# Three stages of a metaformer kernel, their engine programs written without loops

## The reference, cut to what matters

```
x = x + attention(layernorm(x))            # 7x7 windows, shifted, 4 heads
t = t + experts(layernorm(t))              # softmax router over 8 experts, the best 2 mixed
x = x + focal(layernorm(x))                # below
t = t + recurrence(layernorm(t))           # batch norm, then 3136 steps of sigmoid(wx_t + y @ V.T)

experts:  expert_out = einsum('bnd,edc->bnec', x, expert_w) + expert_b
          out = sum over the top 2 of p_k * expert_out[k]
focal:    y = x @ Wf + bf                  # q, context and 4 gates
          three depthwise convolutions with gelu, each times its gate, and a global term
          x_out = q * (ctx_all @ Wh + bh)
          x_out = layernorm(x_out) * gamma + beta
          x_out = x_out @ Wp + bp
```

## Time and profile before

| what | value |
|---|---|
| time, median of 3 runs | 8981.09 us (8978.25 to 9027.3) |
| time of the profiled execution | 8979.28 us |
| its span, first to last instruction | 8977.5 us |
| mean granted TensorE clock | 0.973 |
| PE, DVE, POOL, ACT busy | 90%, 70%, 64%, 50% of the span |
| attention, to 1840 us | 1840 us |
| experts, 1840 to 3862 us | 2022 us |
| focal input, 3862 to 4455 us | 593 us |
| convolution, 4455 to 6070 us | 1615 us |
| focal output, 6070 to 7097 us | 1027 us |
| recurrence, 7097 us to the end | 1880 us |

### The profile page before, as it was taken

One profiled execution on the slowest core, in us unless ns is written; L12 is line 12 of the kernel. 1 busy time (PEld: TensorE's weight loads), 2 busy tenths in 40 slices (PEclk: granted clock), 3 DMA queues, 4 the chain that ended last, 5 costly groups with the idle time before them and its releaser, 6 DMA issues. The chain is left out here.

```text
span 8977.5 us, 330977 instructions
## 1 busy us (share of the span) xinstructions
PE 8051.4 (90%) x112719; PEld 4838.4 (54%) x112719; DVE 6262.3 (70%) x21127; ACT 4513.2 (50%) x12517; POOL 5701.4 (64%) x6959
## 2 busy tenths in 40 slices
PE   7999999978889898779799999988888788888888
PEld 6777777744444444357544444436666555555554
DVE  8999999979999999878656666656777622222222
ACT  5666666645555555469733333335555433333333
POOL 8999999968888888778622222225666644444444
PEclk9999999989999999989999999999999899999999
DMA  1222222211111111258844554538777422222221
GB/s 52 57 57 57 58 58 58 59 53 54 54 54 54 51 53 54 69 183 301 286 163 164 180 181 164 180 124 214 200 203 200 121 55 55 56 56 56 56 55 53
DMA packets 797656, 955.86 MB, mean 106 GB/s; under 512 B 323100, under 2 KB 661825, under 8 KB 773584
## 3 DMA queue, kind: packets, MB, share of 16 engines
q1 hardware_dynamic: 797264, 952.06, 34.7%
HBM read 574.81 MB, written 453.35 MB: 115 GB/s over the span
## 5 line engine op out<-in xcount | busy, mean ns | idle before, releaser
L982 PE MATMUL moe_pe_out<-moe_we,moe_xnT 128*128 128x512 f32 x3136 | 1530.2, 621 | 232.3 <-DVE moe_acc L876 224.9
L1587 PE MATMUL conv_pc<-conv_c,conv_toep 64*64 64x416 f32 (+1 forms) x6896 | 1335.6, 534 | 4.2 <-ACT conv_c L1488 2.7
L778 ACT ACTIVATE moe_scaled<-moe_pe_out,moe_gate 128x128 f32<-128x128 f32 x3136 | 892.5, 368 | 792.8 <-PE moe_pe_out L982 791.1
L2287 ACT ACTIVATE rec_yT<-rec_ph 128x32 f32<-128x32 f32 x3136 | 618.4, 197 | 1251.5 <-PE rec_ph L2408 1251.5
L1443 POOL TENSOR_TENSOR conv_g<-conv_c,conv_gate 128x896 f32<-128x896 f32 x128 | 365.3, 2854 | 1212.2 <-DVE conv_out L1557 1174.6
L982 PEld LDWEIGHTS moe_pe_out<-moe_we,moe_xnT 128*128 128x128 f32 x3136 | 558.5, 195 | 1032.1 <-issue 1023.8
L298 POOL TENSOR_SCALAR att_xn<-att_xin,att_mv,att_rstd 128x128 f32<-128x128 f32 x1024 | 1007.1, 997 | 54.2 <-POOL att_rstd L294 54.2
L2408 PE MATMUL rec_ph<-rec_yT,rec_vt 128*32 128x32 f32 x25080 | 853.1, 207 | 196.6 <-ACT rec_yT L2287 121.8
L2334 DVE COPY rec_xT<-rec_pin 128x512 f32<-128x512 f32 x196 | 135.6, 692 | 1250.5 <-PE rec_pin L2380 1250.5
L2408 PEld LDWEIGHTS rec_ph<-rec_yT,rec_vt 128*32 128x32 f32 x25080 | 506.5, 108 | 647.5 <-ACT rec_yT L2287 609.9
L1587 PEld LDWEIGHTS conv_pc<-conv_c,conv_toep 64*64 64x64 f32 (+1 forms) x6896 | 487.9, 144 | 604.8 <-issue 535.2
(11 more groups left out here) (210 smaller groups left out, 19573.4 us busy)
## 6 DMA issues: line engine op xcount, KB each, us to landing
conv_toep<-rows_dram SPq DMA_DIRECT2D x32, 2304.0 KB, 13.9
c<-foc_cs SPq DMA_DIRECT2D x32, 1792.0 KB, 10.9
conv_cin<-c SPq DMA_DIRECT2D x32, 1792.0 KB, 8.9
ctx_all<-conv_out SPq DMA_DIRECT2D x32, 1792.0 KB, 7.0
att_xin<-x_windows SPq DMA_DIRECT2D x512, 98.0 KB
moe_xin<-x SPq DMA_DIRECT2D x112, 448.0 KB, 3.5
x<-moe_acc SPq DMA_DIRECT2D x112, 448.0 KB, 2.7
foc_xin<-x SPq DMA_DIRECT2D x32, 1568.0 KB, 8.3
```

The costliest lines, as they stand in the source:

```text
L778: ins = act.activation(scaled[:, b, e, :], pe_out[:, b, 1, e * C:(e + 1) * C], ACT.Identity, scale=g)
L982: pe.matmul(pe_out[:, b, half, :], xnT[:, n.slot(2), t, :], we[:, half * 4:half * 4 + 4, :].rearrange("d e c -> d (e c)"), start=True, sto ...
L1587: return pe.matmul(image_pairs(pc[k], half)[m0:m1, :, i0:i1], w, tile[r0:r1, images(half), i0 + away:i1 + away], start=start, stop=(rows ! ...
L2287: act.activation(yT[:, a, cs], ph[:, a, cs], ACT.Sigmoid).then_inc(moved, 1)
```

## The change

The five `run_steps` calls of each of experts, focal input and focal output (15 in all) become calls of a new function that writes every step out. No instruction on data, no wait and no transfer is added, removed or moved within a program; waits and addresses of the former loop steps are constants. `run_steps` stays as it is for the other three stages.

```diff
+def straight_steps(count, unroll, step):
+    for n in range(count):
+        step(Step(0, unroll, n), n, n - count)
...
 # expert_stage: SP, POOL, ACT, DVE, PE
-            run_steps(sp, N, U, step, 5)
+            straight_steps(N, U, step)
...
-            run_steps(pool, N, U, step, 4)
+            straight_steps(N, U, step)
...
 # focal_input_stage: SP, POOL, ACT, DVE, PE
-            run_steps(sp, N, U, step, 4 * NG)
+            straight_steps(N, U, step)
...
-            run_steps(dve, N, U, step, AHEAD)
+            straight_steps(N, U, step)
...
 # focal_output_stage: SP, POOL, ACT, DVE, PE
-            run_steps(sp, N, U, step, 3 * NG)
+            straight_steps(N, U, step)
...
-            run_steps(dve, N, U, step, AHEAD)
+            straight_steps(N, U, step)
```

More of the change, by code:

```diff
@@ L796, in step @@
                         norm(n + 2)
-            run_steps(act, N, U, step, 4)
+            straight_steps(N, U, step)
         @block.vector
@@ L948, in step @@
                     layer_stats_end(n + 3)
-            run_steps(dve, N, U, step, 4)
+            straight_steps(N, U, step)
         @block.tensor
@@ L996, in step @@
                             logits(n + 1, 1)
-            run_steps(pe, N, U, step, 4)
+            straight_steps(N, U, step)
 ROW = 64
@@ L1150, in step @@
                     norm(n + 9, first + 9)
-            run_steps(pool, N, U, step, AHEAD)
+            straight_steps(N, U, step)
         @block.scalar
@@ L1197, in step @@
                 context(n, first)
-            run_steps(act, N, U, step, AHEAD)
+            straight_steps(N, U, step)
         @block.vector
@@ L1309, in step @@
                     turn(n + 8, first + 8)
-            run_steps(pe, N, U, step, AHEAD)
+            straight_steps(N, U, step)
 T_ALL = P * sum(BLOCKS)
```

## The result

The kernel before ran in 8979.67 us (median, 8973.55 to 9027.3), the changed one in 8765.99 us (8764.0 to 8767.61). The ratio is 0.9751, with an interval of 0.9717 to 0.9784: 2.5% faster. I had predicted 8799 us, 8765 to 8850. Applied to the 8981.09 us that the prediction started from, the ratio gives 8757 us. The direction and most of the size were right, and yet the result lies at the low edge of the range or just beyond it: 33 us of gain are missing in my sum.

A forecast was written before the change was run, and what follows sets the result against it. Experts was read as a chain over VectorE; it and focal output stall at loop turns. Terms -85 - 100 + 3 = -182 us on 8979.3 gave 8797, plus 1.8 for the runs' median: 8799 us, range 8765 to 8850.

The forecast's parts named there:

- Experts, -85 predicted: Experts' 100 loop steps: 72.0 us of turn stalls and 15 put to the clock go, taken as 85 us.
- the straight step, 16.58 us: Experts: mean of five prologue and epilogue steps, 16.58 us against 17.45 in the loop, 87 us over 100 steps.
- The stated lower bound of the term, -92: Experts: the most gain allowed, from prologue steps alone, 100 x (17.45 - 16.53) = 92 us.
- The register arithmetic, costed at nothing: Experts, VectorE: 2525 instructions, 101 us of sequencer time, claimed hidden behind VectorE's own data work.
- Focal input, +3 predicted: Focal input: turns cost some 3 us, but straight epilogue steps show no gain; +3 us, bounds -3 and +6.
- ScalarE's copies, at 86%, cover the rest: Focal input: ScalarE's copies, busy 86%, were to hide whatever else the straight code saves.
- Focal output, -100 predicted: Focal output: 25 images fall from 31.71 to 27.7 us, 4.0 each, 100 us less.
- The cautious bound: Focal output: images at 28.7 us, as image 4 in the loop without a turn inside, leaving 75 us of gain.
- Attention, convolution and recurrence as long as before: The three untouched stages were to keep their lengths, a change of 0 us.
- The DMA engines: Rival: they become focal output's bound, images of 28.7 us or more, time 8824 or 8856 us; chance 0.10.
- Straight-code stalls: Second rival, in the three straight stages: a slower kernel, VectorE "issue" waits at regular distances of code; chance 0.03.
- only the branches and their bookkeeping go: Rival: the turn stall is not the fetch and the work only moves; 10 us gained, time 8971; chance 0.03.

The follow-up runs named there:

- dve_straight: Against the kernel before, only VectorE's programs of the three stages written straight, the other four engines keeping their loops; 8778.77 us, ratio 0.9792.
- focal_input_padded_loop: The kernel before with 20 more already met waits (10 instructions) in each step of VectorE's focal input program; that stage took 751.8 us.
- straight_everything: The kernel before with all six stages written straight, no loop left; 8787.44 us, ratio 0.979.
- one_pass_loops: The kernel before with every pass of the three stages' loops made a loop of its own that runs once; 8778.01 us, ratio 0.979.

## Why the prediction was right or wrong

**Experts, -85 predicted, -102.4 measured.** This is the largest miss. The mechanism was right: without VectorE's loop the 72.0 us of stalls are 1.1, and VectorE's program alone gives the whole (dve_straight). The term was mis-sized by the straight step, 16.58 us where 16.43 was measured. I took it from five steps in the prologue and epilogue, and these steps are dearer than the middle's whatever the code: in the changed kernel the same five take 49.4 + 33.4 = 82.8 us, 16.56 each. The stated lower bound of the term, -92, came from prologue steps alone and was no bound for the same reason. So what comes on top of the stalls in the 100 steps is 30.3 us and not the 15 that I gave to the clock.

**The register arithmetic, costed at nothing.** The reason given was that the straight steps are faster by hardly more than the stalls, and it fell with the 16.58. I had also counted 2525 instructions of VectorE, those of L89; with L837 and L887 they are 4600, 184 us of sequencer time. They do run beside VectorE's data work: in the trace of before 4498 of the 4619 ALU_OPs in experts' loop (1951 to 3696 us), 97%, lie wholly in time in which data instructions of VectorE run. Whether that hides all of their price is the question. In focal output nothing was right. In experts a price of up to 30 us is likely, by steps of 16.85 us with the arithmetic and without a turn. No run has it alone, so how the 30.3 us divide between it and the clock stays open.

**Focal input, +3 predicted, -5.2 measured.** The step that failed reads "straight code shows no gain, if anything 0.03 us a step more". The 14 steps of the epilogue (34.6 us) were no sample of straight code. In the changed kernel the same 14 take 34.0, and a step in the middle 2.418 us where the loop's took 2.440. With VectorE alone straight they take 33.9, and with only the others straight 34.65, so the 0.6 us belong to VectorE's program behind its loop and not to the stage's running out. What they are is open. In the loop passes the excess over straight code stands at three of the 14 steps, 0.24 us at the two around the turn and 0.12 ten steps on. At the others loop and straight code agree within 0.03, though the arithmetic stands in all of them. So turns did cost a little here, though the waits that I read as turns were none. "ScalarE's copies, at 86%, cover the rest" did not hold, since the stage gained 5.2 us.

**Focal output, -100 predicted, -98.4 measured.** Right, with its working: 27.78 us an image against the 27.7 taken. Image 2, with all loads and stores beside it, was the sample to trust. The cautious bound (image 4, 28.7) would have missed by 23 us. The stalls were 90.0 us of the gain; beside the rest stands the granted clock, 0.93 in the loop before and 0.50 behind a turn, and 1.00 in the same stretch now. The fetches that the change adds have no term in the sum, and no run shows what hides them. What the changed kernel showed is 348 instruction packets on q14 and 176 on q8, and "issue" entries of VectorE of 1.1 us at most in experts' stretch, 5.0 (as before) in focal input's and 0.7 in focal output's.

**Recurrence, 0 predicted, -10.7 measured.** "Attention, convolution and recurrence as long as before" failed. This term was not in the sum at all. A change of one stage's code moves every stage behind it, and TensorE's loop had stood on a bad place. The slow turns stood in the trace of before, in the intervals of the recurrence; I did not look there, as the stage was untouched. That the change would take them away could not be read from it.

**Together.** The terms missed by 17.4 (experts), 8.2 (focal input) and 10.7 (recurrence), less 1.6 in focal output: 34.7 us, against 33 between 8799 and 8766. The range allowed 13 us for straight steps that are faster in the middle of a stage than near its ends; the two terms that rest on such steps missed by 25.6. I had named the right weakness and given it half its size.

**Why a turn costs 3 us or 8.** The prediction gave the difference to data in the DMA queues. The case fits it: 3.0 us with the DMA engines at 16%, 5.9 to 6.7 at 59% (focal_input_padded_loop), 7.5 at 78%. So do the packets: in the trace of before the first instruction packet behind VectorE's branch starts 0.9 to 1.2 us after it in experts and 3.0 to 6.5 us in focal output (medians 0.95 and 5.48). But no run changed the data alone, so it is not shown that the data make it late.

**The rivals.** The DMA engines did rise, to 91% in focal output, and did not become the bound: images take 27.78, not 28.7. Straight-code stalls did not appear in the three stages: the "issue" waits left are the 1.1, 5.0 and 0.7 us above. Code without any loop is slower elsewhere, by 21 us in straight_everything; whether by late code is not shown. That only the branches and their bookkeeping go, for 10 us, is refuted by the gain of 214 us; and one_pass_loops, which still has a branch in each pass and never takes it back, has nearly all of that gain.

## What to carry to other kernels

Count the instructions between two branches of each engine, and look at the first wait behind the branch: a body of 282 on VectorE turned for 0.25 us, one of 353 or more for 3 to 9, and doubling a body that is already too long saved next to nothing in experts, where the turn grew, and 64 us in focal output. Write straight only the program of the engine that stalls (here VectorE's gave all of it in its stages); code without loops everywhere was slower. Take the price of a straight step from the middle of a stage where there is one, not from its ends. Look in the trace whether an experiment left in the code what it was meant to keep. And price an edit that adds or removes many instructions also for the loops behind it: 12 instructions of nothing took 10 us off the recurrence.

## What the runs showed of the hardware that I had not expected

- The price of a turn depends on where the loop lies: focal output's turn grew by a second stall of 2.8 us (976.2 to 1022.3 us) when 5 instructions a step were added in another stage, and not when 10 were.
- TensorE's loop in the recurrence, whose body is kept (4 instruction packets in all from 7250 to 8950 us), still paid 0.10 us a turn for one place about ten instructions behind its beginning. 12 instructions ahead of it took that away.
- Waits that are already met were not free where VectorE is busy 82% of the time: 10 instructions a step, most of 0.050 us, cost 0.55 us a step in focal input (655.4 against 531.8 us).
- The issue of a transfer on SyncE took 0.42 us in straight code and 0.33 in the loop (medians in the recurrence), with single ones of 2.3 us; in experts it took 0.320 in straight code and 0.345 in the loop.
- A branch in each pass that is not taken back cost nothing that shows: focal output 878.0 us with it, 877.8 without.
